# One VectorE instruction over two PSUM banks for the row maxima of the first layer

## The chip, the cores and the metric

The kernel runs on one core of one Trainium2 chip. The metric is the device time of one execution in microseconds, the median of several runs. The core has a matmul engine (TensorE, PE in the profile), a vector engine (VectorE, DVE), a scalar engine (ScalarE, ACT), a general one (GpSimd, POOL) and SyncE (SP), which issues most transfers. Matmul results land in PSUM, eight banks of 512 float32 numbers for each of 128 partitions. Each engine works through its own instructions in order; semaphores order the engines among each other.

## The reference, cut to what matters

Input x is 8 batches of 512 tokens of width 128. Two layers follow one another; each is attention, multiplied by a gate that a mixture of experts gives, and added to x:

```
x  = x0
xn = layernorm(x);  s = attention_0(xn);  g = silu(experts_0(xn));  x = x + s * g
xn = layernorm(x);  s = attention_1(xn);  g = silu(experts_1(xn));  x = x + s * g
```

attention_0 has 16 heads of width 8 with no mask: 8 heads on the first half of xn, 8 on a smoothed copy of the second input (a fixed linear map over time, the Holt smoothing), each a softmax over 512 keys, then a projection, two layer norms and a feed-forward part. attention_1 has 16 causal heads with a linear bias. A softmax needs, for each query row and head, the maximum of 512 scores before the exponentials.

## The kernel before, in words

Attention goes in batch steps b = -2 to 16 (`batches`, `plan`), written out as a list of named steps that all engines follow in the same order. In a step b the kernel makes three kinds of work side by side. First, the **scores** of batch b: a score unit is one head's transposed scores, keys by queries, one 128 x 512 matmul into a bank (L582), an exponential of it by ScalarE (L771), and, for every four units, a sum over keys by eight matmuls (L623). Second, the **maxima** of batch b + 1: a max unit is one head and one tile of 128 query rows, a 128 x 512 matmul into a bank (L589), and a `tensor_reduce` by VectorE that writes the negated maximum of the 512 numbers into one column of `neg_max` (L876). The maxima are later carried into the operands of the next batch's scores (`minus`, `shift`). Third, **other steps**: projections, transposes, layer norms, feed-forward, routing, gathers. They share one bank, `ps_misc`.

In the first layer a batch has 64 score units and 64 max units (`UNITS[0]`), one of each in every `unit` step. Max units 2k and 2k + 1 of a half are the same tile of query rows, for a head of the upper set (j = 1) and its partner in the lower set (j = 0) (`max_unit`). First-layer maxima are made in the eight batch steps b = -1 to 6, those of b = -1 without scores beside them; experts_0 runs between b = 0 and b = 1, experts_1 much later. `plan` puts the sums and the other steps behind units of even number (`(place + 1) * units <= (u + 2) * PLACES`, with 64 units and 32 places; sums stand at u = 4g + 6). So on TensorE an odd unit and the even one after it follow one another with nothing between them, and the sum and the other steps come behind that.

Banks: 0 to 2 are a ring for the scores, 3 to 5 a ring for the maxima (`RING` = 3, `MAX_BANK` = 3), 6 holds the sums, 7 is `ps_misc`. In b = -1 the maxima have banks 2 to 5. TensorE takes the bank of max unit n (n counts over all batches) when `max_out` has reached n - 2, which says that unit n - 3 is reduced: `wait(pe, sems["max_out"], n.at("max_out") - ahead)`, `ahead` = 2; in b = -1 `ahead` is 3. This wait stands in front of both matmuls of the `unit` step, the score's too. VectorE waits for `max_in` to reach n + 1, reduces, and raises `max_out` by 1. `adds` is the table by which every engine counts the semaphores' values as the list goes on.

Of the kernel before, what the change touches and what calls it, by code (L numbers as in the profile page):

```python
# [10 lines left out]
ALU = mybir.AluOpType  # L11
ACT = mybir.ActivationFunctionType
AX = mybir.AxisListType
# [4 lines left out]
QT = S // P  # L18
# [105 lines left out]
def wait(eng, sem, value):  # L124

    if value > 0:
        eng.wait_ge(sem, value)
# [10 lines left out]
BANKS, RING, MAX_BANK, SUM_BANK, MISC_BANK = 8, 3, 3, 6, 7  # L138
# [102 lines left out]
    return half, j, [(first + k, 1, 0, 2 * P, 2 * P * k) for k in range(2)]  # L241


def sums_of(layer):


    if layer == 0:
        return {4 * g + 3: g for g in range(H)}
    return {10 * u + last: 3 * u + k for u in range(QUADS) for k, last in enumerate((3, 7, 9))}
# [88 lines left out]
def adds(step):  # L338

    name, d, arg, layer = step  # L340
    both = {"misc": 1, "misc_free": 1}
    if name == "unit":
        return {**({"scores": 1, "probs": 1} if arg[0] is not None else {}), **({"max_in": 1, "max_out": 1} if arg[1] is not None else {})}
    if name == "fetch":
        return {f"strips{arg[0]}": 16 * (4 + 4 * arg[1])}
    table = {
        "load": {"z_in": 16}, "loadx": {"x_in": 16}, "sum": {"summed": 1}, "take": {"taken": 1},
        "norm": {**both, "dve": 1}, "zTa": {}, "zT": both,
        "q": {**both, "split": 1, "pool": 3, "q_out": 16 * PARTS}, "k": {**both, "split": 1, "pool": 3, "k_out": 16 * PARTS},
        "v": both, "z": both, "shift": {**both, "shift_in": 64}, "minus": {"dve": 1, "minus": 1},  # L350
        "onT": both, "yT": both, "ff1": both, "x2T": both, "logits": both,
        "proj": both, "pmom": {"dve": 1, **({"moments": 1, "rstd": 1, "pool": 1} if arg == 1 else {})},
        "fmom": {"dve": 1, **({"moments": 1, "rstd": 1, "pool": 1} if arg == 1 else {})},
        "ln1": {"pool": 3, "y": 1, "yb": 1}, "ff2a": {},
        "ff2": both,
        "ln2": {"pool": 2, "s": 1}, "gather": {"rows": 16 * QT * (1 if layer == 0 else TOP)},
        "gate": {"gate_in": 1, "pool": 0 if layer == 0 else 1}, "tanh": {"gate_tanh": 1}, "gz": {"gate_out": 1},
        "mix": {"pool": 1, "x2": 1}, "store": {"x2_out": 16}, "tail_take": {"tail_taken": 1},
        "tail_norm": {"tail_norm_in": 1, "tail_norm": 1, "dve": 1}, "tail_turn": {"tail_turn_in": 1, "tail_turn": 1},
        "tail_out": {"tail_out_in": 1, "tail_free": 1, "x2": 1, "x2_out": 16},  # L360
        "ln3a": {"dve": 1, "moments": 1, "rstd": 1, "pool": 1}, "ln3b": {"xn2": 1},
        "gates": {}, "rstd0": {}, "choose0": {}, "count0": {}, "scan0": {}, "slots0": {}, "weigh0": {}, "send0": {}, "wide": {}, "fold": both,
        "positions": {}, "masks": {}, "rest": {}, "choose": {}, "count": both, "place": {}, "weigh": {}, "send": {},
    }
    return table[name]
# [17 lines left out]
def attention(nc, const, psum, banks, strips, tokens, xn2, work, dram, weights, routes, out, setup_of, experts_of):  # L383


    with ExitStack() as ctx:
# [58 lines left out]
        with nc.Block() as block:  # L445
# [76 lines left out]
            def _(pe):  # L522
                n = Tally(adds)
# [26 lines left out]
                for b, steps in batches():  # L550
# [12 lines left out]
                    for step in steps:  # L563
# [3 lines left out]
                        if name == "unit":  # L567
# [4 lines left out]
                            half, jm, max_pieces = max_unit(mi, max_layer) if mi is not None else (0, 1, [])  # L572

                            ahead = RING - 1
                            if b == -1:
                                mbank, ahead = banks[:, 2 + n.at("max_in") % 4, :], 3
                                if mi == 0:
                                    setup["logits_ready"](pe)

# [251 lines left out]
            def _(dve):  # L831
# [20 lines left out]
                for b, steps in batches():  # L852
# [10 lines left out]
                    for step in steps:  # L863
# [3 lines left out]
                        linked[0] = 0  # L867
                        if name == "unit" and arg[1] is not None:
                            _, mi, max_layer = arg
                            bank = banks[:, 2 + n.at("max_in") % 4 if b == -1 else MAX_BANK + n.at("max_in") % RING, :]  # L870
                            half, j, pieces = max_unit(mi, max_layer)
                            slot, qt, *_ = pieces[0]
                            hd, e = QT * j + slot % QT, mi % 10
                            wait(dve, sems["max_in"], n.at("max_in") + 1)
                            if max_layer == 0:
                                dve.tensor_reduce(neg_max[:, half, qt, hd:hd + 1], bank, AX.X, ALU.max, negate=True).then_inc(sems["max_out"], 1)  # L876
                            else:

                                wait(dve, sems["max_out"], n.at("max_out") - 1)
                                for i, (_, qt, lo, hi, at) in enumerate(pieces):  # L880
                                    best = neg_max[:, half, qt, hd + (i if e >= 8 else 0):hd + (i if e >= 8 else 0) + 1]
                                    op = dve.tensor_tensor_reduce(masked[:, n.at("max_in") % 2, at:at + hi - lo], bank[:, at:at + hi - lo],  # L882
                                                                  const["mask_wide"][:, S - (hi - lo):S], -1.0, BIG, ALU.add, ALU.min, best)
                                op.then_inc(sems["max_out"], 1)
# [1218 lines left out]
```

## Time and profile before

| | |
|---|---|
| median of 3 runs | 1211.7 us (1206.21 to 1215.12) |
| profiled execution, its own time | 1209.44 us |
| its span, first to last instruction | 1207.6 us |
| mean granted TensorE clock | 0.912 |
| PE busy | 1022.9 us, 7484 matmuls |
| DVE busy | 794.5 us, 2469 instructions |
| ACT busy | 649.1 us |
| POOL busy | 577.0 us |
| reduces of L876 | 512, 323.8 us busy, 681 ns each |

A line of the profile names the source line, the engine, the tile written and the tile read. "Idle before" is the time for which the engine sat idle just ahead of the instruction, with what released it. A busy share is an average: an engine that is busy two thirds of the time can still be what another engine waits for at a given place.

### The profile page before, as it was taken

How to read it: one execution, taken by the hardware profiler on the slowest of the kernel's cores; microseconds unless marked ns; L12 is line 12 of the kernel's file. 1: busy time of each engine (PE TensorE's matmuls, PEld its weight loads, DVE VectorE, ACT ScalarE, POOL GpSimd, SP SyncE). 2: the span in 40 equal slices, each digit the busy share in tenths (PEclk: the TensorE clock that was granted, in tenths of full speed). 3: DMA queues.
4: the chain of work that ended last, by engine and by line, in shares of the span. 5: the costliest groups of instructions: out<-in, count | busy, mean ns of one | idle time of the engine just before them, and what ended most of it. 6: DMA issues, size and time to landing. Idle time of an engine off the chain costs nothing. (4 is left out here: it accounts for less than half of the span.)

```text
span 1207.6 us, 22982 instructions
## 1 busy us (share of the span) xinstructions
PE 1022.9 (85%) x7484; PEld 547.3 (45%) x7484; DVE 794.5 (66%) x2469; ACT 649.1 (54%) x1255; POOL 577.0 (48%) x670
## 2 busy tenths in 40 slices
PE   4888589998989898887887877786999998899797
PEld 2622149733333333332333343444899754454343
DVE  5597463488878787877776565765444486788631
ACT  1204352376757676665675544444444476677665
POOL 5274500064637373728758578643000165455654
PEclk8657699999999999997998887878999999999978
DMA  5852337681404050412422224124788644354221
GB/s 143 233 136 61 95 114 215 187 210 39 105 22 116 6 128 15 102 31 63 100 62 69 49 64 104 40 79 122 228 254 245 182 109 104 81 136 109 69 53 44
DMA packets 122552, 130.53 MB, mean 108 GB/s; under 512 B 13968, under 2 KB 105424, under 8 KB 122224
## 3 DMA queue, kind: packets, MB, share of 16 engines
q1 hardware_dynamic: 115872, 116.09, 37.0%
q0 software_dynamic: 6144, 12.60, 4.1%
q8 instruction: 58, 0.95, 0.3%
q10 hardware_dynamic: 432, 0.52, 0.2%
q14 instruction: 46, 0.38, 0.1%
HBM read 83.13 MB, written 52.48 MB: 112 GB/s over the span
## 5 line engine op out<-in xcount | busy, mean ns | idle before, releaser
L876 DVE TENSOR_REDUCE a_neg_max<-ps_banks 128x1 f32<-128x512 f32 x512 | 323.8, 681 | 88.2 <-PE ps_banks L589 70.6
L771 ACT ACTIVATE a_probs<-ps_banks 128x512 f32<-128x512 f32 x512 | 279.2, 599 | 154.5 <-PE ps_banks L582 138.1
L582 PE MATMUL ps_banks<-q_strip,k_strip 53*128 53x512 bf16 (+3 forms) x1024 | 281.5, 356 | 74.0 <-DVE a_neg_max L876 30.9
L589 PE MATMUL ps_banks<-k_strip,q_strip 51*128 51x512 bf16 (+3 forms) x1024 | 301.7, 364 | 20.5 <-DVE a_neg_max L876 17.0
L882 DVE CUSTOM_DVE_ANT_0 a_masked<-ps_banks,mask_wide 128x384 bf16<-128x384 f32 (+3 forms) x512 | 223.8, 487 | 91.4 <-PE ps_banks L589 73.4
L773 ACT ACTIVATE a_probs<-ps_banks 128x512 f32<-128x512 f32 x256 | 144.5, 600 | 82.2 <-PE ps_banks L540 69.8
L1062 POOL DMA_INDIRECT tokens<-made,at x96 | 93.3, 972 | 177.6 <-DMA made<-work 126.6
L582 PEld LDWEIGHTS ps_banks<-q_strip,k_strip 53*128 53x128 bf16 x1024 | 72.2, 95 | 164.9 <-issue 62.6
L623 PE MATMUL ps_banks<-a_probs,v_aug 128*32 128x512 f32 x1024 | 143.6, 634 | 0.4
L589 PEld LDWEIGHTS ps_banks<-k_strip,q_strip 51*128 51x128 bf16 x1024 | 74.1, 95 | 142.8 <-ACT a_probs L771 57.8
L1988 POOL DMA_INDIRECT sent<-xn,at x64 | 62.4, 975 | 41.5 <-DMA sent<-xn,at 24.0
L1021 POOL CAST a_q_parts<-a_q_whole 128x512 bf16<-128x512 f32 x16 | 9.8, 610 | 150.3 <-ACT a_q_whole L812 150.3
L539 PE MATMUL ps_banks<-mask_kq,ident_halves 64*128 64x256 bf16 (+1 forms) x320 | 80.1, 262 | 0.3 <-issue 0.3
L1787 PE MATMUL ps_banks<-work 128*128 128x256 f32 x320 | 78.7, 390 | 0.3 <-DMA work<-in_pack 0.2
L1970 DVE SCALAR_TENSOR_TENSOR work<-ps_banks,work 128x256 f32<-128x256 f32 x80 | 35.0, 479 | 64.8 <-ACT work L1824 56.5
L628 PE MATMUL ps_banks<-a_probs,v_aug 128*32 128x512 f32 (+2 forms) x768 | 76.9, 507 | 0.1
L540 PE MATMUL ps_banks<-mask_kq,ident_halves 64*128 64x128 bf16 (+1 forms) x320 | 66.0, 212 | 0.1
L1824 ACT ACTIVATE work<-ps_banks,work 128x256 f32<-128x256 f32 x80 | 33.5, 470 | 56.8 <-PE ps_banks L1787 56.7
L1787 PEld LDWEIGHTS ps_banks<-work 128*128 128x128 f32 x320 | 58.8, 194 | 7.8 <-DMA work<-in_pack 0.9
L775 ACT ACTIVATE a_probs_c<-ps_banks 128x512 f32<-128x512 f32 x64 | 36.5, 595 | 29.2 <-PE ps_banks L540 22.0
L909 DVE RECIPROCAL a_o_den<-ps_banks 128x16 f32<-128x16 f32 x63 | 16.0, 254 | 49.8 <-PE ps_banks L634 35.8
L720 PE MATMUL ps_banks<-work,w_ff 128*128 128x256 f32 x128 | 39.3, 433 | 8.6 <-ACT work L816 5.0
(258 smaller groups left out, 1719.3 us busy)
## 6 DMA issues: line engine op xcount, KB each, us to landing
work<-in_pack SPq DMA_DIRECT2D x40, 450.0 KB, 3.5
q_rows<-a_q_parts SPq DMA_DIRECT2D x96, 128.0 KB
k_rows<-a_k_parts SPq DMA_DIRECT2D x96, 128.0 KB
q_strip<-q_rows SPq DMA_DIRECT2D x64, 192.0 KB
k_strip<-k_rows SPq DMA_DIRECT2D x64, 192.0 KB
work<-in_w SPq DMA_DIRECT2D x32, 256.0 KB, 3.1
sent<-in_zeros SPq DMA_DIRECT2D x14, 512.0 KB, 7.9
work<-sent SPq DMA_DIRECT2D x56, 128.0 KB, 3.3
```

Of the source, the lines that this page charges most:

```text
L539: return pe.matmul(blocks, half_ident(j, half), triangle, start=False, stop=last)
L540: return pe.matmul(blocks[:, :, to], half_ident(j, half), triangle[:, :, src], start=False, stop=last)
L582: mm = pe.matmul(sbank[:, at:at + hi - lo], k_now[rows(js, ROW_END), slot, kt * P:(kt + 1) * P], q_now[rows(js, ROW_END), slot, lo:hi], st ...
L589: mm = pe.matmul(mbank[:, at:at + hi - lo], q_next[rows(jm, ROW_SHIFT), slot, qt * P:(qt + 1) * P], k_next[rows(jm, ROW_SHIFT), slot, lo:h ...
L623: mm = pe.matmul(out_of[c], v_of[k][c], probs[group % 2][:, c, :], start=k == 0, stop=k == QT - 1)
L628: mm = pe.matmul(out_of[c][:, lo:S], v_of[kt][c], kept[:, c, at:at + S - lo], start=kt == 0, stop=kt == 2)
L771: act.activation(probs[si // 4 % 2][:, si % 4, :], bank, ACT.Exp).then_inc(sems["probs"], 1)
L773: act.activation(probs[e // 4][:, e % 4, :], bank, ACT.Exp).then_inc(sems["probs"], 1)
L876: dve.tensor_reduce(neg_max[:, half, qt, hd:hd + 1], bank, AX.X, ALU.max, negate=True).then_inc(sems["max_out"], 1)
L882: op = dve.tensor_tensor_reduce(masked[:, n.at("max_in") % 2, at:at + hi - lo], bank[:, at:at + hi - lo], const["mask_wide"][:, S - (hi - ...
L1062: pool.indirect_dma_start(rows[:, t, :], None, moe[layer], bass.IndirectOffsetOnAxis(ap=routes[layer]["at"][i][:, QT * at + t:QT * at + t ...
L1787: mm = pe.matmul(hidden_bank(par, i)[:, c, :], pack[par][:, (i * FC1 + c) * P:(i * FC1 + c + 1) * P], rows_T[par][:], start=True, stop=True)
```

## The change

In the first layer the even max unit of a pair is no longer reduced when it is written. At the odd unit one `tensor_reduce` reads both banks (128 x 2 x 512) and writes two columns of `neg_max`, four apart, and raises `max_out` by 2. With a ring of three banks the pairs fall on banks (3, 4), (5, 3) and (4, 5) in turn; the pair on (5, 3) keeps its two single reduces (`apart`), and the first of these raises nothing. In b = -1 the pairs lie on (2, 3) and (4, 5), and all are taken together. On TensorE, `ahead` becomes 0 for the odd unit of a pair: it waits until all pairs before its own are reduced. The even unit waits until the pair before the last is reduced, since `max_out` now grows at odd units alone. In b = -1 `ahead` is 2 for both. The second layer's maxima are as before.

```diff
--- before.py
+++ after.py
@@ -239,6 +239,11 @@
     if e < 8:
         return half, j, [(slot, 2, 0, 3 * P, 0), (slot, 0, 0, P, 3 * P)]
     return half, j, [(first + k, 1, 0, 2 * P, 2 * P * k) for k in range(2)]
+
+
+def paired(arg):
+
+    return arg[1] is not None and arg[2] == 0
 
 
 def sums_of(layer):
@@ -340,7 +345,7 @@
     name, d, arg, layer = step
     both = {"misc": 1, "misc_free": 1}
     if name == "unit":
-        return {**({"scores": 1, "probs": 1} if arg[0] is not None else {}), **({"max_in": 1, "max_out": 1} if arg[1] is not None else {})}
+        return {**({"scores": 1, "probs": 1} if arg[0] is not None else {}), **({"max_in": 1, "max_out": 2 * (arg[1] % 2) if paired(arg) else 1} if arg[1] is not None else {})}
     if name == "fetch":
         return {f"strips{arg[0]}": 16 * (4 + 4 * arg[1])}
     table = {
@@ -572,8 +577,10 @@
                             half, jm, max_pieces = max_unit(mi, max_layer) if mi is not None else (0, 1, [])
 
                             ahead = RING - 1
+                            if paired(arg) and mi % 2 == 1:
+                                ahead = 0
                             if b == -1:
-                                mbank, ahead = banks[:, 2 + n.at("max_in") % 4, :], 3
+                                mbank, ahead = banks[:, 2 + n.at("max_in") % 4, :], 2
                                 if mi == 0:
                                     setup["logits_ready"](pe)
 
@@ -867,15 +874,23 @@
                         linked[0] = 0
                         if name == "unit" and arg[1] is not None:
                             _, mi, max_layer = arg
-                            bank = banks[:, 2 + n.at("max_in") % 4 if b == -1 else MAX_BANK + n.at("max_in") % RING, :]
+                            bank = banks[:, MAX_BANK + n.at("max_in") % RING, :]
                             half, j, pieces = max_unit(mi, max_layer)
                             slot, qt, *_ = pieces[0]
                             hd, e = QT * j + slot % QT, mi % 10
-                            wait(dve, sems["max_in"], n.at("max_in") + 1)
-                            if max_layer == 0:
-                                dve.tensor_reduce(neg_max[:, half, qt, hd:hd + 1], bank, AX.X, ALU.max, negate=True).then_inc(sems["max_out"], 1)
+                            at = 2 + n.at("max_in") % 4 if b == -1 else MAX_BANK + n.at("max_in") % RING
+                            if paired(arg):
+                                second = mi % 2 == 1
+                                apart = (MAX_BANK + RING - 1 == at and not second or MAX_BANK == at and second) and b >= 0
+                                if second or apart:
+                                    wait(dve, sems["max_in"], n.at("max_in") + 1)
+                                    if apart:
+                                        op = dve.tensor_reduce(neg_max[:, half, qt, hd:hd + 1], banks[:, at, :], AX.X, ALU.max, negate=True)
+                                    else:
+                                        op = dve.tensor_reduce(neg_max[:, half, qt, QT + slot % QT::-QT], banks[:, at - 1:at + 1, :], AX.X, ALU.max, negate=True)
+                                    op.then_inc(sems["max_out"], 2) if second else None
                             else:
-
+                                wait(dve, sems["max_in"], n.at("max_in") + 1)
                                 wait(dve, sems["max_out"], n.at("max_out") - 1)
                                 for i, (_, qt, lo, hi, at) in enumerate(pieces):
                                     best = neg_max[:, half, qt, hd + (i if e >= 8 else 0):hd + (i if e >= 8 else 0) + 1]
```

## Rows read from the trace of the kernel before

**Rows 1.** The profile's page: busy time by engine; the chain that ended last, by engine.

```profile
PE 1022.9 (85%) x7484; PEld 547.3 (45%) x7484; DVE 794.5 (66%) x2469; ACT 649.1 (54%) x1255; POOL 577.0 (48%) x670
...
PE 19%; issue 4%; DVE 3%; POOL 3%; ACT 1%; DMA 1%; another core or an unknown queue 1%; POOLq 0%; SPq 0%; ACTq 0%; DVEq 0%
```

**Rows 2.** Busy time by stage, its columns first: steps b = -1, 0, 2.

```profile
core 0: us, PE busy (x) PEld busy (x) DVE busy (x) ACT busy (x) POOL busy (x), PEclk, DMA share, GB/s
45.60:100.00 54.40, 41.07 (x104) 12.06 (x104) 48.63 (x91) 4.70 (x7) 32.70 (x37) 0.59 0.60 171
101.00:167.00 66.00, 49.33 (x300) 14.31 (x300) 42.29 (x74) 37.97 (x72) 25.88 (x28) 0.82 0.33 92
...
292.20:356.60 64.40, 57.97 (x390) 23.75 (x388) 51.52 (x120) 43.31 (x82) 35.35 (x38) 0.97 0.29 67
```

**Rows 3.** Waits of step b = 2: waiter <- releaser: us in total, times, longest.

```profile
PEld ps_banks L589 <- ACT a_probs L771: 6.1, 13, 0.8
PEld ps_banks L582 <- ACT a_probs L771: 5.4, 5, 1.7
...
PE ps_banks L582 <- DVE a_neg_max L876: 2.6, 4, 1.1
```

**Rows 4.** VectorE's instructions grouped by line and shape: busy us, mean ns | idle before.

```profile
L876 DVE TENSOR_REDUCE a_neg_max<-ps_banks 128x1 f32<-128x512 f32 x512 | 323.8, 681 | 88.2 <-PE ps_banks L589 70.6 <-remote 10.1 <-issue 4.3
L882 DVE CUSTOM_DVE_ANT_0 a_masked<-ps_banks,mask_wide 128x512 bf16<-128x512 f32 x128 | 84.9, 687 | 36.5 <-PE ps_banks L589 31.7 <-issue 4.0
...
L882 DVE CUSTOM_DVE_ANT_0 a_masked<-ps_banks,mask_wide 128x256 bf16<-128x256 f32 x128 | 47.7, 420 | 22.8 <-PE ps_banks L589 15.8 <-issue 5.2 <-remote 1.6
...
L1123 DVE TENSOR_REDUCE work<-work 128x32 f32<-128x512 f32 x1 | 0.7, 676 | 0.0
```

**Rows 5.** Timeline, step b = -1: start us, us, instruction, count [idle before].

```profile
83.47 6.66 DVE L876 TENSOR_REDUCE a_neg_max<-ps_banks 128x1 f32<-128x512 f32 x11
```

**Rows 6.** Timeline, TensorE and VectorE: one clean pass, then one release.

```profile
273.29 0.39 PE L589 MATMUL ps_banks<-k_strip,q_strip 51*128 51x512 bf16 x1
...
273.71 1.29 DVE L876 TENSOR_REDUCE a_neg_max<-ps_banks 128x1 f32<-128x512 f32 x2 [1.31 <-PE ps_banks L589]
...
319.50 0.68 DVE L876 TENSOR_REDUCE a_neg_max<-ps_banks 128x1 f32<-128x512 f32 x1
...
320.32 0.37 PE L589 MATMUL ps_banks<-k_strip,q_strip 51*128 51x512 bf16 x1 [0.21 <-DVE a_neg_max L876]
```

**Rows 7.** Timeline, TensorE, step b = 2: first and last odd max matmul of 32.

```profile
293.12 0.39 PE L589 MATMUL ps_banks<-k_strip,q_strip 51*128 51x512 bf16 x1
...
356.44 0.39 PE L589 MATMUL ps_banks<-k_strip,q_strip 51*128 51x512 bf16 x1
```

**Rows 8.** Timeline, TensorE, step b = 2: odd max matmuls between 316 and 324.

```profile
316.78 0.39 PE L589 MATMUL ps_banks<-k_strip,q_strip 51*128 51x512 bf16 x1
...
317.90 0.39 PE L589 MATMUL ps_banks<-k_strip,q_strip 51*128 51x512 bf16 x1
...
319.44 0.39 PE L589 MATMUL ps_banks<-k_strip,q_strip 51*128 51x512 bf16 x1
...
322.24 0.39 PE L589 MATMUL ps_banks<-k_strip,q_strip 51*128 51x512 bf16 x1
...
323.37 0.39 PE L589 MATMUL ps_banks<-k_strip,q_strip 51*128 51x512 bf16 x1
```

**Rows 9.** Timeline, VectorE and TensorE, end of step b = 2.

```profile
350.50 0.39 PE L589 MATMUL ps_banks<-k_strip,q_strip 51*128 51x512 bf16 x1
350.73 0.59 PE L589 MATMUL ps_banks<-k_strip,q_strip 51*128 51x512 bf16 x2
...
351.71 5.85 DVE L876 TENSOR_REDUCE a_neg_max<-ps_banks 128x1 f32<-128x512 f32 x9
...
352.54 0.37 PE L582 MATMUL ps_banks<-q_strip,k_strip 53*128 53x512 bf16 x1 [1.21 <-ACT a_probs L771]
```

**Rows 10.** Waits of TensorE between 120 and 143 us.

```profile
PE ps_banks L582 <- issue: 9.8, 3, 6.3
```

## The prediction

> **What bounds the kernel now.** I read the page first. PE is busy for 85% of the span, VectorE for 66%, and the chain that ended last runs mostly through PE and hardly through VectorE [rows 1]. So a saving on VectorE is worth only what it gives where PE waits for VectorE. Then I read busy time by stage. Step b = 2, typical of b = 1 to 6, takes 64.4 us: PE 58.0, VectorE 51.5, ScalarE 43.3. Step b = -1 has no scores: VectorE has 48.6 of 54.4 us and PE 41.1 [rows 2]. So VectorE leads in one short step, and PE in the long ones. Third, the waits of b = 2. PE waits there for VectorE's reduces for only 2.6 us; its weight loads wait 11.5 us (6.1 + 5.4) for exponentials [rows 3]. Last, the timeline of single passes, to see how far apart the odd max matmuls stand, since the change hangs a new wait on them.
>
> **What the merge saves on VectorE.** A single reduce takes 681 ns; a custom pass over PSUM takes 687 ns for 512 numbers and 420 for 256 [rows 4], so 256 numbers cost 267 ns, and 512 cost 534. A reduce of 1024 should take 681 + 534 = 1215 ns (estimate). No reduce over two banks is in the trace. The cheap bound is this one; the dear one is two full reduces, 1362 ns. I take 1215, as a reduce into 32 results takes 676 ns for 512 numbers [rows 4], so further rows of results cost nothing.
>
> The saving is less than 1362 - 1215 = 147 ns, however. Eleven reduces in a row take 6.66 us [rows 5]: the last lasts 0.68, so ten spacings take 5.98, 0.60 us each, and each reduce starts 0.08 before the one in front ends. Two cost 1.21 us of the queue and the merged one 1.215 - 0.08 = 1.14: 0.07 us saved. The Trainium skill (VectorE: DVE Perf Modes, The DRAIN you can't avoid) says that the next op does not start until the pipe has emptied. By that rule the saving would be the full 0.147. The trace disagrees: its starts are 0.60 apart and the duration 0.68.
>
> Merged are all 32 pairs of b = -1. Of the 224 pairs of b = 0 to 6 the 74 on banks 5 and 3 stay single and 150 are merged. VectorE's saving is 182 x 0.07 = 13 us in all. On the path lies b = -1 alone, 32 x 0.07 = 2.3 us, if everything behind it moves up too. Bounds there: nothing, as step b = 0 has a stall in which PE waits up to 6.3 us at once with nothing on VectorE or ScalarE that releases it [rows 10], which may swallow the gain; and 32 x 0.147 = 4.7. I take 2. The looser or tighter waits of b = -1 (four banks, two pairs) cost nothing as long as PE refills two banks inside the 1.14 us of the other pair; if not, a few tenths per pair, at most some 5 us.
>
> **What the new wait costs.** Today the even unit may be reduced while PE does something else, and a bank comes free three units later. After the change the next odd unit waits until the pair before it is wholly reduced, and that reduce can't begin before the last odd matmul is through. The loop from one odd max matmul to the next is therefore: matmul start to reduce start 0.42 us (273.29 to 273.71), the reduce of both banks 1.215, and the release: a reduce ends at 319.50 + 0.68 = 320.18 and the matmul starts at 320.32, 0.14 [rows 6]. Sum 1.78 us. For a pair left single the loop is 0.42 + 0.68 + 0.14 = 1.24. These are floors; the score matmul of the odd unit stands behind the same wait, and the even unit, the sum and all other steps stand behind it on PE. ScalarE, which waits for scores, and GpSimd and the SP queue, fed by `ps_misc` steps, get everything later.
>
> Now the spacings of today. In b = 2 there are 32 odd max matmuls, at 293.12 first and 356.44 last [rows 7], so 63.3 / 31 = 2.04 us apart on average, above the floor. But they are uneven. Between 316.78 and 323.37 they are 1.12, 1.54, then (with the one at 320.32 of [rows 6]) 0.88, 1.92 and 1.13 apart [rows 6, 8]. The floors there, by bank, are 1.78, 1.78, 1.24, 1.78, 1.78: shortfalls 0.66, 0.24, 0.36, 0 and 0.65, 1.9 us. Over all 31 spacings of b = 2 I count 10 under their floor, 5.9 us short. The same count gives 5.5, 6.9, 5.5, 4.4 and 7.3 for b = 1 and 3 to 6, together 35.5 us, and 6.9 for the part of b = 0 behind its stall: 42.4 us. What is short before the stall I cost at nothing, as the stall hides it; without that cover it is 2 to 3 us more.
>
> Not all of it stays. At the end of b = 2 two odd units are 0.45 apart (350.50 and the second of the two at 350.73), 1.33 us short, but PE then waits 1.21 us for an exponential [rows 9], and a PE that comes later waits less. In the stretch of [rows 8] no such wait is left and 1.9 us stay. If I let every gap between PE's matmuls take up lateness that has piled up, walking through the seven steps leaves 15 us; if about a third is taken up, as in these two samples together, 27 us. I take the middle, 21, since some of the gaps are waits on chains that move along. Bounds: 0 and 42.
>
> Other VectorE work delays the pair's reduce (norm, z, moments, about ten pieces of 0.3 to 0.7 us in a step); most stand in the long spacings, so I cost them at nothing, bounded by 1 us per step, 6 us.
>
> **The two rules on grouping.** In b = 2 VectorE is busy 80% of the stage and a queue of nine reduces back to back exists [rows 2, 9], yet PE seldom waits for it. The Trainium skill (Perfetto Trace Analysis, Optimizing Scalar/DVE Operations) says that grouping helps when the engine is saturated, and that where it is not but causes bubbles on others, breaking up instructions may let work finish sooner. Its first half speaks for the change and describes the second rival; the second half speaks against it and describes my forecast.
>
> **Sum.** 1209.4 us, the profiled execution's own time (span 1207.6), - 2 + 21 = 1228.4. The median of the runs stood 2.3 above that execution, so I forecast 1231 us.
>
> **Rivals.** *Absorbed.* PE's 11.5 us of waits for exponentials per step [rows 3] exceed the 5.9 us short; if ScalarE sets the pace, later scores cost nothing as long as ScalarE has one in hand. For it: the ends of the steps [rows 9]. Against it: in [rows 8] the spacing is shorter than 1.24 because PE has nothing to wait for. Time: 0 to 10 us over, 1210 to 1222. Chance 0.22.
>
> *VectorE is the limit after all.* The mechanism: in stretches where reduces run back to back (nine in 5.85 us [rows 9]), VectorE's queue sets PE's pace, and a shorter queue lets PE go on. The price is 0.07 us for a merged pair, 13 us in all: 1198 us. It decides where the queue of VectorE, other work included, is longer than 1.78 us per pair, since the loop above is then hidden. At 51.5 us per 32 pairs [rows 2] it is 1.61 on average, so only in parts. By the skill's rule on the drain, in the part above, the saving would be 27 us and the time 1185. Chance 0.12, 0.09 of it over 1% faster.
>
> *Nothing is taken up.* ScalarE starves when the odd unit's score comes late and pushes its own lateness on, and other VectorE work lengthens the loop: 42 + 6 - 0 = 48 us at most, 1245 to 1260. Chance 0.16.
>
> *The merged instruction does not do what it says,* that is, two banks cost like two reduces: loop 1.93 instead of 1.78, some 4 us more. It is inside the range.
>
> **How the numbers follow.** The forecast, 1222 to 1245, has 0.50. The range 1207 to 1252 takes in the absorbed case and half of the last; about 0.1 lies under it and 0.08 over it. A measurement of this kernel can tell about 1% (12 us) from no change: 1199.6 to 1223.8 is "same". Faster 0.09; same 0.27 (0.20 absorbed, 0.03 from the faster case, 0.04 from the forecast's edge); slower 0.64.
>
> **What the profile after would show.** L876 has 330 instructions, 182 of them with a mean near 1.21 us; if near 1.36, the saving is wrong. Spacings of odd max matmuls are hardly ever under 1.24, and under 1.78 only at single pairs; waits of L582 and L589 for L876 in b = 2 rise from 2.6 us to 6 or more, waits for exponentials fall. Steps b = 1 to 6 are each 2 to 5 us longer, b = -1 1 to 2 shorter, experts_0, experts_1 and the second layer the same. If the steps keep their length while the waits rise, the work was absorbed. If waits for L876 fall, I am wrong from the start.

## The result, and the profile after

The changed kernel takes 1257.6 us (median of 4 runs, 1256.9 to 1259.4) against 1213.4 for the kernel before: ratio 1.0377, 95% interval 1.033 to 1.0424. It is 44 us slower; I had forecast 19 (-2 + 21).

The page after, first part and the two groups of the first layer's reduces:

```profile
PE 1029.8 (82%) x7484; PEld 556.1 (44%) x7484; DVE 783.6 (62%) x2287; ACT 653.1 (52%) x1255; POOL 577.5 (46%) x670
...
L890 DVE TENSOR_REDUCE a_neg_max<-ps_banks 128x2 f32<-128x1024 f32 x182 | 220.6, 1222 | 123.0 <-PE ps_banks L596 107.4
...
L888 DVE TENSOR_REDUCE a_neg_max<-ps_banks 128x1 f32<-128x512 f32 x148 | 100.8, 683 | 18.5 <-PE ps_banks L596 14.7
```

They answer to [rows 1, 4]. The instruction does what it says: 182 merged reduces of 1.222 us, against my 1.215, and VectorE has 10.9 us less to do, against my 13. Its idle time ahead of these reduces has grown from 88.2 us [rows 4] to 141.5 (123.0 + 18.5), and the part of it that a max matmul ended from 70.6 to 122.1: VectorE waits more and works less.

Busy time by stage in the changed kernel (columns as in [rows 2]): steps b = -1, 0, 2, then b = 1 to 6 together, then all that follows the first layer's maxima:

```profile
45.60:95.00 49.40, 28.64 (x104) 9.81 (x103) 46.35 (x60) 4.70 (x7) 32.24 (x37) 0.60 0.67 190
96.30:173.00 76.70, 49.28 (x300) 15.32 (x300) 41.14 (x51) 38.90 (x72) 25.91 (x28) 0.82 0.30 84
...
305.50:379.30 73.80, 61.94 (x390) 24.65 (x388) 50.84 (x98) 43.76 (x82) 34.30 (x36) 0.89 0.27 62
...
237.30:672.20 434.90, 357.72 (x2310) 146.24 (x2312) 302.01 (x576) 262.03 (x492) 223.63 (x249) 0.93 0.30 72
...
672.60:1257.00 584.40, 505.05 (x4240) 304.66 (x4236) 351.88 (x1463) 322.67 (x638) 275.29 (x333) 0.91 0.43 113
```

The same two long stretches in the kernel before, which were not among the rows ahead:

```profile
231.50:620.30 388.80, 343.58 (x2310) 139.09 (x2312) 309.23 (x704) 258.74 (x492) 219.83 (x246) 0.97 0.34 81
...
620.70:1207.00 586.30, 499.99 (x4238) 301.79 (x4235) 352.65 (x1463) 322.88 (x638) 278.69 (x336) 0.92 0.43 113
```

These rows show where the 50 us between the two spans lie. Steps b = 1 to 6 grew from 388.8 to 434.9, 46 us. Step b = 0 grew by 10 to 11, b = -1 shrank by 4 to 5, experts_0 is as it was, and everything behind is 2 us shorter. The granted clock in b = 1 to 6 fell from 0.97 to 0.93.

Waits of step b = 2 in the changed kernel (as [rows 3]):

```profile
PE ps_banks L596 <- DVE a_neg_max L890: 6.8, 8, 1.9
PE ps_banks L596 <- DVE a_neg_max L888: 2.1, 2, 1.3
...
PEld ps_banks L596 <- ACT a_probs L778: 15.0, 16, 2.4
...
ACT a_probs L778 <- PE ps_banks L589: 21.7, 18, 2.8
```

PE's waits for reduces rose from 3.0 us (the 2.6 of [rows 3] and 0.4 at L589) to 8.9. The weight loads' waits for exponentials, which I had expected to fall, rose from 11.5 to 15.0 us. A part of these 15.0 us belongs to the same places: at 364.7 us the weight load's wait of 1.70 is put down to an exponential, and the wait of the matmul behind it, 1.34, to a reduce. ScalarE's waits for score matmuls rose to 21.7 us; in the kernel before they were

```profile
ACT a_probs L771 <- PE ps_banks L582: 13.9, 14, 2.6
```

One pass of the loop in the changed kernel, first the line of VectorE, then PE's timeline:

```profile
332.07 1.23 DVE L890 TENSOR_REDUCE a_neg_max<-ps_banks 128x2 f32<-128x1024 f32 x1 [0.20 <-PE ps_banks L596]
```

```profile
331.58 0.39 PE L596 MATMUL ps_banks<-k_strip,q_strip 51*128 51x512 bf16 x1
...
333.44 0.37 PE L596 MATMUL ps_banks<-k_strip,q_strip 51*128 51x512 bf16 x1 [0.67 <-DVE a_neg_max L890]
...
335.29 0.37 PE L596 MATMUL ps_banks<-k_strip,q_strip 51*128 51x512 bf16 x1 [0.25 <-DVE a_neg_max L890]
336.61 0.37 PE L596 MATMUL ps_banks<-k_strip,q_strip 51*128 51x512 bf16 x1 [0.71 <-DVE a_neg_max L888]
```

The odd max matmul starts at 331.58, the merged reduce at 332.07 (0.49 later) and ends at 333.30, and the next odd max matmul starts at 333.44, 0.14 after. That is a spacing of 1.86; the next is 1.85, and 1.32 where the pair is reduced by single instructions. In steps b = 0 to 6 no spacing is under 1.31 us, while in the kernel before they went down to 0.44. The floors of my forecast were 1.78 and 1.24. The difference is the start of the reduce after its matmul: 0.42 in the kernel before (63 of its 186 spacings), 0.48 to 0.49 here; no run shows why.

Of the signs that I had named, the 330 reduces, the floors and the stages that changed are there. But steps b = 1 to 6 are each 6 to 9 us longer, not 2 to 5.

### The profile page after: what moved, and what is told of

It reads as the page before. It is cut to its first block and busy times, and to the rows that moved or that the text cites. A ratio compares the mean times of both kernels' runs of the same rounds, so it can differ in the third digit from the quotient of the medians.

```text
span 1257.5 us, 23049 instructions
## 1 busy us (share of the span) xinstructions
PE 1029.8 (82%) x7484; PEld 556.1 (44%) x7484; DVE 783.6 (62%) x2287; ACT 653.1 (52%) x1255; POOL 577.5 (46%) x670
## 5 line engine op out<-in xcount | busy, mean ns | idle before, releaser
L596 PE MATMUL ps_banks<-k_strip,q_strip 51*128 51x512 bf16 (+3 forms) x1024 | 290.7, 370 | 117.3 <-DVE a_neg_max L890 79.8
L589 PE MATMUL ps_banks<-q_strip,k_strip 53*128 53x512 bf16 (+3 forms) x1024 | 280.9, 362 | 32.3 <-DVE a_neg_max L897 14.7
L890 DVE TENSOR_REDUCE a_neg_max<-ps_banks 128x2 f32<-128x1024 f32 x182 | 220.6, 1222 | 123.0 <-PE ps_banks L596 107.4
L630 PE MATMUL ps_banks<-a_probs,v_aug 128*32 128x512 f32 x1024 | 150.4, 662 | 0.0
L589 PEld LDWEIGHTS ps_banks<-q_strip,k_strip 53*128 53x128 bf16 x1024 | 74.9, 95 | 108.9 <-ACT a_probs L780 52.0
L888 DVE TENSOR_REDUCE a_neg_max<-ps_banks 128x1 f32<-128x512 f32 x148 | 100.8, 683 | 18.5 <-PE ps_banks L596 14.7
L2003 POOL DMA_INDIRECT sent<-xn,at x64 | 62.6, 978 | 44.4 <-DMA sent<-xn,at 26.9
```

The source lines that it names most:

```text
L589: mm = pe.matmul(sbank[:, at:at + hi - lo], k_now[rows(js, ROW_END), slot, kt * P:(kt + 1) * P], q_now[rows(js, ROW_END), slot, lo:hi], st ...
L596: mm = pe.matmul(mbank[:, at:at + hi - lo], q_next[rows(jm, ROW_SHIFT), slot, qt * P:(qt + 1) * P], k_next[rows(jm, ROW_SHIFT), slot, lo:h ...
L630: mm = pe.matmul(out_of[c], v_of[k][c], probs[group % 2][:, c, :], start=k == 0, stop=k == QT - 1)
L888: op = dve.tensor_reduce(neg_max[:, half, qt, hd:hd + 1], banks[:, at, :], AX.X, ALU.max, negate=True)
L890: op = dve.tensor_reduce(neg_max[:, half, qt, QT + slot % QT::-QT], banks[:, at - 1:at + 1, :], AX.X, ALU.max, negate=True)
```

## The experiments

They ran on chips of two speeds: the kernel before takes 1170 us on the faster ones and 1213 to 1226 on the others, where PE stalls in b = 0 for some 17 us that the faster ones do not lose. So ratios are told, each against the kernel before on its own chip, and stage times are given for b = 1 to 6, which take the same time on both (386.0 and 388.8 us in the kernel before). A stage time comes from the one profiled execution of a kernel, a ratio from all its executions. Columns: "at half clock" is the time in b = 1 to 6 for which the granted clock stood at 1.2 GHz. The theories: **1**, the loop from an odd max matmul over the reduce of the pair to the next odd max matmul makes the loss; **2**, putting reduces off to the odd unit costs by itself; **3**, the instruction over two banks is to blame; **4**, scores held behind the wait starve ScalarE; **5**, the granted clock; **6**, other VectorE work in the loop.

| kernel | ratio, 95% interval | b = 1 to 6, us | at half clock in it, us |
|---|---|---|---|
| before (c0) | 1 | 386.0 | 20.5 |
| changed (first comparison) | 1.0377, 1.033 to 1.0424 | 434.8 | 59.5 |
| changed again (c1) | 1.0411, 1.034 to 1.0483 | 435.1 | 61.4 |
| e1 release by pair | 1.0067, 1.0036 to 1.0098 | 393.6 | 20.5 |
| e2 two at odd | 1.0347, 1.0292 to 1.0402 | 433.1 | 70.8 |
| e3 first step only | 0.9996, 0.9971 to 1.0021 | 388.4 | 27.3 |
| e4 score ahead | 1.0279, 1.0229 to 1.0329 | 417.0 | 35.4 |
| e5 four banks, merged | 1.035, 1.0309 to 1.039 | 418.2 | 47.8 |
| e6 four banks, single | 1.0125, 1.0095 to 1.0155 | 391.2 | 10.2 |
| e7 half read, merged | 0.9902, 0.9864 to 0.9941 | 387.5 | 27.3 |
| e9 half read, single | 0.9875, 0.9822 to 0.9928 | 386.7 | 20.5 |
| e10 four banks, aligned, merged | 1.0243, 1.0191 to 1.0296 | 399.0 | 10.2 |
| e11 four banks, aligned, single | 1.0261, 1.0197 to 1.0325 | 396.6 | 13.7 |
| e15 score ahead again | 1.0267, 1.0233 to 1.0302 | 417.0 | 35.4 |
| e12 filler | 1.0317, 1.0281 to 1.0353 | 420.7 | 23.9 |
| e8 first step, score ahead | 0.9972, 0.9953 to 0.9992 | 386.3 | 20.5 |
| changed, third time (c2) | 1.0407, 1.0352 to 1.0462 | 434.8 | 55.6 |
| e16 more VectorE work, merged | 1.0667, 1.0606 to 1.0728 | 466.4 | 85.3 |
| e17 more VectorE work, single | 1.0227, 1.0174 to 1.028 | 423.7 | 44.4 |

**c0, c1, c2: the two kernels again.**

> The kernel before, unchanged, for its profile beside the other kernels of this call on the same chip. All theories: the same time as the runs of before, steps b = 1 and 2 from first to last max matmul 60.5 and 63 to 64 us.

> The changed kernel, unchanged, timed on the chip of these experiments, so that its ratio and its stage times stand beside theirs. Theory 1 (the loop): the same 1.035 to 1.04 as in the first comparison; the step b = 0 has no stall on this chip, and nothing in the theory hangs on that stall. Rival: a part of the first loss belonged to the stall, 1.02 to 1.03 here.

> The changed kernel, unchanged, as the base of e16 on this chip: 1.035 to 1.04 of before.

c0 took 1166.5 us in its one execution; seven others of the kernel before on that chip took 1169.2 to 1175.2, so it is 0.4% under their median. c1 and c2 gave 1.0411 and 1.0407; c1 ran on the slower chips. e2, which differs from the changed kernel by 0.06 us a pair, gave 1.0347 where b = 0 has no stall, so the loss does not hang on the stall.

**e1: single reduces, release by pairs.** In the changed kernel's VectorE part:

```diff
+ wait(dve, sems["max_in"], n.at("max_in") + 1)
+ op = dve.tensor_reduce(neg_max[:, half, qt, hd:hd + 1], banks[:, at, :], AX.X, ALU.max, negate=True)
+ op.then_inc(sems["max_out"], 2) if second else None
- (single or merged reduce, at the odd unit)
```

> Every max unit is reduced by its own instruction as soon as it is written, as in the kernel before; TensorE's waits and the release of banks by pairs are those of the changed kernel. The loop from one odd max matmul to the next is then 0.48 + 0.68 + 0.15 = 1.31 us for all pairs, where the changed kernel shows 0.48 + 1.22 + 0.15 = 1.85. Theory 1, the length of the loop makes the loss: spacings of the kernel before fall under 1.31 by some 2 to 3 us in a step, so 1213 + 10 to 20, 1223 to 1235, and no spacing under 1.31. Theory 2, releasing by pairs is what costs, whatever the reduce takes: 1250 or more. Theory 3, the single reduce over two banks is to blame and nothing else: 1213.

1.0067, 7.2 us by the medians, b = 1 to 6 7.6 us longer than c0; least spacing 1.32. Theory 2 in its form "release by pairs costs whatever the reduce takes" falls, and so does theory 3 in its strict form, which had 1 here. Theory 1's range was 10 to 20 us, a little high.

**e2: both maxima at the odd unit, by two instructions.**

```diff
- op = dve.tensor_reduce(neg_max[:, half, qt, QT + slot % QT::-QT], banks[:, at - 1:at + 1, :], AX.X, ALU.max, negate=True)
+ if not apart:
+     dve.tensor_reduce(neg_max[:, half, qt, hd + QT:hd + QT + 1], banks[:, at - 1, :], AX.X, ALU.max, negate=True)
+ op = dve.tensor_reduce(neg_max[:, half, qt, hd:hd + 1], banks[:, at, :], AX.X, ALU.max, negate=True)
```

> The changed kernel with its merged instruction taken apart again: both maxima of a pair are reduced at the odd unit by two instructions back to back, 0.60 + 0.68 = 1.28 instead of 1.22 us. Waits, order and release stay as changed. Theory 1 (loop length) and theory 2 (release by pairs): as slow as the changed kernel or a little slower, 1258 to 1270, of which about 2 to 3 in step b = -1 and 0.06 for each of about 85 pairs whose loop binds. Theory 3 (the instruction over two banks is to blame): 1213 to 1225.

1.0347. The merged instruction is not to blame: without it the loss is the same. Busy time of b = 1 to 6, one row each from c0, e1 and e2 (us of the stretch, PE, weight loads, VectorE, ScalarE, GpSimd, clock):

```profile
214.60:600.50 385.90, 343.20 (x2308) 139.30 (x2308) 308.27 (x704) 258.85 (x492) 220.15 (x246) 0.97 0.34 82
```

```profile
213.30:606.90 393.60, 340.61 (x2308) 140.38 (x2308) 308.96 (x704) 260.26 (x492) 221.07 (x246) 0.97 0.33 80
```

```profile
221.80:655.00 433.20, 362.22 (x2310) 146.06 (x2310) 308.02 (x703) 261.73 (x492) 223.25 (x249) 0.92 0.30 73
```

VectorE is busy for 308 to 309 us in all three, with 703 or 704 instructions. Only when the reduces may start differs, and that is worth 40 us between e1 and e2 in these profiles. By the medians it is 35 us, since the profiled execution of e2 was the slowest of its four (1220.1 us, median 1212.9).

**e3: merged in b = -1 alone.** `paired` asks for `arg[0] is None` as well, and b = 0 to 6 are as before.

> The merged instruction in step b = -1 alone, where there are four banks and no scores; from b = 0 on everything is as in the kernel before. In the changed kernel b = -1 is 4.4 us shorter from its first to its last max matmul. If step b = 0 takes that over: 1209, 4 to 5 us less than before. If the stall in the middle of b = 0 (GpSimd sends tokens out one after another) swallows it: the same as before within 1 us. Either way the whole loss is in b = 0 to 6.

0.9996: nothing that this run can tell, which is about 3 us. The 4.4 us by which b = -1 was shorter in the first profile are not the merge's either: b = -1 took 52.8 us before, 48.3 in the first profile after, 53.4 in c1 and 53.6 in c2 (between its first and last max matmul), and 49.9 in c0 against 49.0 in e3.

**e4, e15: the score's matmul ahead of the wait.**

In the changed kernel both matmuls of a unit stand behind the wait. In e4 and e15 (the lines that matter):

```diff
+ if early:                       # a score and a first-layer maximum in the unit
+     score_piece(0)
  wait(pe, sems["max_out"], n.at("max_out") - ahead)
+ if early:
+     max_piece(0)
```

> The changed kernel with one order turned: in a first-layer unit TensorE issues the score's matmul before it waits for the bank of the maxima, so that the score is not held behind that wait. Theory 4, the loss is made worse by ScalarE running dry behind the held scores (its waits for scores rose from 13.9 to 21.7 us in step b = 2): 1240 to 1250. Theory 1 alone (loop of maxima): 1255 to 1258, since the odd max matmuls keep their floor of 1.85 us and set the pace.

> e4 (changed kernel, score's matmul ahead of the wait for the maxima's bank) once more, as the control of e12 on the same chip: 1.025 to 1.03 of before, and TensorE at half clock for some 40 us of steps b = 1 to 6.

1.0279 and 1.0267, inside what theory 4 had expected: b = 1 to 6 take 417.0 us instead of 434.8, so 18 us come back in the stages. By the medians it is less: e4 is 9.6 us faster than e2 on the same chip. ScalarE's waits for scores in b = 2 are 19.3 instead of 21.7 us, and time at half clock fell from 60 to 35 us. The edit does a second thing: the spacings behind merged pairs now sit on a floor of 1.77 to 1.81 instead of 1.85, as the max matmul starts 0.06 us after the reduce's end and not 0.15. Counted as in my prediction, the spacings of the kernel before are 34.9 us under floors of 1.77 and 1.24, and 40.0 under 1.85 and 1.32; so some 5 of the 18 us may be the shorter loop and not the earlier score (estimate).

**e5, e6: four banks for the maxima, two for the scores.** In both `sbank = banks[:, n.at("scores") % 2, :]`, `mbank = banks[:, 2 + n.at("max_in") % 4, :]`, `wait(pe, sems["probs"], n.at("probs") - 1)`; e5 merges all pairs (`ahead = 2`), e6 none (`ahead = 3`).

> The changed kernel with four banks for the maxima in every step (banks 2 to 5, as in b = -1) and two for the scores (0 and 1). All pairs are merged, and a unit waits for the pair before the last, not for the last. Theory 1, the loop: the floor is 1.85 us for two pairs, that is 0.93 a pair, and no longer binds; what is left is the price of the missing score bank, which e6 measures by itself. e5 and e6 are then within 1% of each other. Theory 2, reduces put off to the odd unit cost by themselves (they stand behind other VectorE work, and the maxima are ready later): e5 is slower than e6 by 2% or more.

> The kernel before with the same banks as e5: two for the scores, four for the maxima, each unit reduced by itself and released by itself. It measures the price of the missing score bank: a score waits for the exponential two units before it. Theory of scores that run dry: 3% or more slower than before. Otherwise, as four banks for the maxima give back some of PE's waits for reduces (2.6 us in a step): within 1%.

1.035 and 1.0125. By my expectation the distance between them spoke for theory 2; e6 by itself lies between the 1% and the 3% that I had put down for it. But the floor that I had written down for e5 was wrong. PE's timeline of e5 at the end of step b = 3:

```profile
417.23 0.37 PE L586 MATMUL ps_banks<-q_strip,k_strip 53*128 53x512 bf16 x1 [1.07 <-DVE a_neg_max L887]
...
419.25 0.60 PE L593 MATMUL ps_banks<-k_strip,q_strip 51*128 51x512 bf16 x1
```

The matmul that waits at 417.23 is the score of an even unit, and it waits for a reduce. The even unit 2k + 2 follows the odd unit 2k + 1 at once and needs the bank of pair k - 1, whose odd half was written one burst earlier. So the loop binds there too, at another place. The matmul at 419.25 takes 0.60 us, where [rows 6] have 0.39 for the same: the granted clock has fallen (the profile has it at 1.2 GHz from 417.8 us on).

**e10, e11: the same banks, and other steps behind odd units.** `(place + 1) * units <= (u + 1) * PLACES` for all steps, and sums four units after their last exponential instead of three.

> e5 with another order of steps: sums and other steps stand behind odd units instead of even ones, so that both units of a pair follow one another on TensorE. In e5 the even unit that follows an odd one waits for the pair that the odd unit of the burst before completed, so the loop of 1.85 us still stood between bursts, in spite of four banks. Here a burst waits for the pair of the burst before the last. Theory 1 (the loop): e10 and e11 within 0.5% of each other. Theory 2 (a reduce put off costs by itself, as VectorE idles for half of the pair): e10 is slower than e11 by 1 to 2%, as e5 than e6 (1.035 and 1.0125).

> e6 with the order of steps of e10: the control without the merge. The order itself may cost or give something against e6 (1.0125): the score behind each burst now has two exponentials to wait for at once, so 1.01 to 1.03.

1.0243 and 1.0261; b = 1 to 6 take 399.0 and 396.6 us, and 2.2 of the 2.4 us between them lie in b = 6. In step b = 3 the 31 spacings of the two kernels are the same to 0.01 us but for one, 2.76 against 2.87, though all pairs are merged in one and none in the other. With the loop out of the way a reduce put off to the odd unit costs nothing that these runs can tell (to some 0.5%); theory 2 falls here. Both kernels lose 2.5% to the order and the missing score bank, most of it outside these steps.

**e7, e9: half of each bank is read,** `0:S // 2` in place of the whole bank, in the changed kernel and in the kernel before.

> The changed kernel, but each reduce of the first layer reads 256 of the 512 scores of a bank, so the maxima are those of half of the keys. The merged reduce then takes 0.68 us, as a single one did, and the loop 0.48 + 0.68 + 0.15 = 1.31 us as in e1, while the reduces are still put off to the odd unit and still stand behind other VectorE work. Theory 1, length of the loop: as e1, ratio 1.00 to 1.01. Theory 2, the order on VectorE: the loss stays to a good part, 1.02 or more.

> The kernel before, but each reduce of the first layer reads 256 of the 512 scores of a bank, so the maxima are those of half of the keys. It is the control for e7 (changed kernel, half read, 0.990): it has the short reduces without the merge and without the wait. If VectorE's own time matters in the kernel before (its reduces now 0.42 instead of 0.68 us), 0.98 to 0.985, and then e7's put-off reduces still cost 0.5 to 1%. If it hardly matters apart from step b = -1: 0.99, the same as e7, and with a loop of 1.31 us the merge costs nothing.

0.9902 and 0.9875. A merged reduce of 2 x 256 numbers (0.690 us) makes the loop as short as e1's, and b = 1 to 6 take 387.5 us merged and 386.7 single, as much as the kernel before. The merge, the waits by pairs and the order on VectorE are all there in e7; only the length of the loop is not. The shorter reduces lighten VectorE too, but they do so in both kernels, which end up alike. The ratio under 1 is not the loop's: in e7 step b = -1 takes 41.0 us against 49.9 in c0, which is about what e7 gains; e9 gains 15 us, of which its b = -1 (46.2 us) explains a part, and the rest was not placed.

**e12: filler in the waits.** e15 with the score's matmul of odd units issued three times from unit 47 of a step on.

```diff
+ for _ in range(2 if mi % 2 == 1 and mi >= 47 else 0):
+     pe.matmul(sbank, ...)       # the same product, before score_piece(0)
```

> e15 with filler on TensorE: from max unit 47 of a first-layer step on, the score's matmul of the odd unit is issued three times instead of once, into the same bank, before the wait (the last one counts; the result is the same). That is 54 times 0.43 us or more of TensorE work in places where it mostly waits. Theory 5, a part of the loss is the granted clock, which falls to half where TensorE idles in the loop: less time at half clock in steps b = 1 to 6 and a ratio 0.005 to 0.01 below e15. Theory 1 alone, or a clock that does not follow idling: the filler is hidden or costs, e15 plus 0 to 10 us, and the time at half clock stays.

1.0317 against 1.0267 for e15. Time at half clock fell from 35.4 to 23.9 us, and still the kernel is no faster. That is neither of the two outcomes that I had written down. In step b = 3 one spacing fell from 2.64 to 1.77, where the clock had been at half, and three rose, 2.52 to 2.95 the most, where the filler was not hidden. The filler did change the time at half clock, but the run doesn't price it. A rough price comes from two profiles of the same kernel: step b = 3 of the changed kernel took 68.9 us in the first and 70.7 in c1,

```profile
379.30:448.40 69.10, 58.57 (x390) 24.27 (x386) 48.37 (x91) 43.76 (x82) 33.57 (x36) 0.97 0.26 59
```

```profile
381.70:452.50 70.80, 60.95 (x390) 24.55 (x388) 48.51 (x91) 43.73 (x82) 33.81 (x36) 0.91 0.27 60
```

with 4.7 and 12.8 us at half clock: 1.8 us for 8.1, about 0.22 a microsecond. The executions on record say the same: among those of one kernel on one chip, 148 in 23 groups, the time rises by 0.21 us for each microsecond at half clock, taken from their mean granted clocks. For the 39 us more at half clock (59.5 against 20.5) that is some 8 us of the 46, an estimate, and neither source tells whether the clock made an execution longer or the longer waits lowered the clock.

**e16, e17: more VectorE work,** `dve.tensor_reduce(spare[i][:], ps_misc, AX.X, ALU.max)` ahead of norm, z, proj and ff2 in b = 1 to 6.

> The changed kernel with seven more VectorE instructions in each of steps b = 1 to 6: a reduce of ps_misc (0.6 us of VectorE's queue) into one spare column ahead of norm (4), z, proj and ff2; the results don't change. 4.2 us a step, 25 in all. Theory 6: other VectorE work that stands ahead of a pair's reduce lengthens the loop of 1.85 us and reaches TensorE one to one where the loop binds (95 of 186 spacings), and this made some 26 us of the measured loss. Then e16 is slower than c2 by 13 to 25 us, and clearly more than e17 is slower than before. Rival: VectorE has slack and the loss is the bare loop: e16 and e17 rise alike, by less than 8 us.

> The kernel before with the same seven instructions a step. It measures what they cost where each unit is reduced and released by itself: the ring of three takes up much of it. Theory 6: 1.003 to 1.01 of before (4 to 12 us), less than in the changed kernel. Rival: the same rise as in e16.

1.0667 and 1.0227: by the medians 30 us more than c2, and 25 more than before. In b = 1 to 6 it is 31.6 and 34.9 us. Neither kernel takes up any of the added 25 us. The added work stands ahead of the release of `ps_misc`, for which PE waits in either kernel, so it tests that release too and not the pair's alone. Theory 6, that other VectorE work weighs more in the changed kernel, is not confirmed; e17's 4 to 12 us was plainly wrong, and e16's 13 to 25 was too low.

**e8: the harmless parts alone,** e3 and e4's edits on the kernel before.

> The kernel before with the two parts that did no harm by themselves: merged reduces in b = -1 (e3: 0.9996) and the score's matmul ahead of the wait for the maxima's bank (worth 0.7% in the changed kernel, e4 against c1). TensorE waits for reduces for only 2.6 us in a step of the kernel before, so at most 1 us a step comes back: 0.993 to 1.00. Rival: the score ahead of the odd max matmul delays the maxima and VectorE: 1.00 to 1.005.

0.9972, 0.9953 to 0.9992: 3 to 4 us faster than the kernel before. As e3 gave nothing, it is likely the score's place; the two parts were not told apart at this size.

## Why the prediction was wrong

The direction, the mechanism and its place were right: the loop, its floor, the steps in which it binds, and the other stages unchanged. What the merge saves on VectorE was nearly right too (10.9 us less busy for my 13, none of it on the path). The size was off by 2.3 times, and the time lies above the range. The reading of the chain in [rows 1] carried nothing: in the kernel before that chain goes back to 818.6 us only, behind all of the first layer's maxima, so it says nothing of the steps in which the change acts.

**The step that failed is what becomes of the count: "Not all of it stays", 21 us taken off, while other VectorE work ahead of the pair's reduce, "I cost them at nothing", put nothing against it.** The count itself was nearly right. With the measured floors 1.85 and 1.32 instead of 1.78 and 1.24 the same spacings of b = 1 to 6 come 40.0 us short instead of 35.5, and the measured growth of their spacings is 42.9, where half of 35.5 was forecast. So, as a net, all of it stays. The net has parts. In the first profile after, 95 of the 186 spacings are released by a reduce (release within 0.2 us); their reduces start 25.8 us later in sum than 0.49 after their matmul, 11.5 of it in b = 5. Against that, spacings that are shorter after than before make 23.2 us: 40.0 + 25.8 - 23.2 is 42.6. I had bounded the first at 6 us. What was taken up, 23.2, is not less than the 18 that I took off in these steps. One such late start, at the end of b = 2:

```profile
359.25 0.39 PE L596 MATMUL ps_banks<-k_strip,q_strip 51*128 51x512 bf16 x1
...
360.90 0.46 DVE L1373 CAST ident_halves<-consts 64x128 bf16<-64x128 f32 x2
361.39 1.23 DVE L890 TENSOR_REDUCE a_neg_max<-ps_banks 128x2 f32<-128x1024 f32 x1
```

The pair's reduce could start at 359.74 and starts at 361.39, behind seven other VectorE instructions (L945, L1366 to L1373).

**The cause of the size stays open in part.** The late starts alone are not enough: in e1, by the same count, 68 spacings start 25.9 us late in sum, as much as in the changed kernel, and c0's spacings are 19.7 us short of a floor of 1.32 for all pairs, yet e1's grow by 6.5 us only against c0. There 33 us are taken up by shorter spacings, in the changed kernel 23 of a larger sum. By these counts the longer loop does two things that I did not put together: it raises more spacings to its floor, and it leaves less room to make up for them. e16 and e17 do not show that added VectorE work costs the changed kernel more than the one before.

The sample that I took for recovery was the end of b = 2, where PE waited 1.21 us for an exponential [rows 9]. The six last spacings of each step, of 31, hold 18.3 of the 42.9 us: the ends of the steps lose most. PE's wait for ScalarE there was not slack, at least in part because the score that ScalarE needed next stood behind the same wait as the maxima. e4 speaks for that: with the score ahead these last spacings grow by 11.0 us instead of 18.3, though e4's loop is also a little shorter.

**Step b = 0** lost 10.8 us in the first comparison, 9.6 without the stall (e2 against c0), where I had counted 6.9 short and nothing for the part ahead of the stall; with the measured floors the whole step comes 10.6 short. The stall did not hide that part. **The gain of 2 us in b = -1** was not seen, though e3 could not have told 2 us from none.

**The clock** had no term in my sum. It is about 8 us by the estimate above; in e12 the time at half clock fell and the kernel was no faster, so it stays an estimate.

**The rivals.** "Nothing is taken up" (0.16, 1245 to 1260) has the time that came, and both things that it names are there: ScalarE waits longer for scores, and other VectorE work delays the pair's reduce. Its number is in part luck: it had 42 + 6 - 0, and the trace has 40.0 + 25.8 - 23.2 for b = 1 to 6. "Absorbed" and "VectorE is the limit" are out by e1, e2 and e7. The Trainium skill (Perfetto Trace Analysis, Optimizing Scalar/DVE Operations) had it in the half that speaks against the change: where an engine is not saturated but makes others wait, breaking up instructions may let work finish sooner. The runs agree: e1, where each unit is reduced as it comes, has 40 us less in b = 1 to 6 than e2, where both wait for the odd unit. By the rule that I took from the Trainium skill (VectorE: DVE Perf Modes, The DRAIN you can't avoid) merging would have freed 0.147 us of VectorE a pair. I had read that section too narrowly: it also says that an op that is not held starts earlier, and the starts 0.60 us apart [rows 5] agree with that. Measured is 10.9 us over 182 pairs, 0.06 a pair; neither size shows in a time, as no saving of VectorE reached the path.

## What to carry to other kernels

When an instruction is merged over several buffers of a ring, count the loop that the ring has left: producer start to consumer start, the whole merged consumer, and the release. Compare it with the shortest spacings of the producer, not with their mean. The shortfall is no fixed price: of 40 us short all stayed here, of the 20 us of e1's shorter loop about a third. So take all of it as lost for a loop near the mean spacing (1.85 against 2.05), unless a trace shows that what stands behind the same wait has slack of its own. If a merge is wanted, it needs a second full set of buffers, and the producer's bursts must match the merged group, as in e10, where the merge then cost nothing; but that kernel was 2.4% slower than before, by the bank and the order that it took. If something must wait, put the work that others need ahead of the wait.

## What the runs showed of the hardware

- A max reduce over two PSUM banks in one instruction takes 1.222 us for 2 x 512 float32 numbers, 0.683 for 512 in one bank; 2 x 256 numbers over two banks take 0.690 (e7). So the second bank costs next to nothing beyond its numbers.
- From the odd max matmul's start to the start of an idle VectorE's reduce is 0.48 to 0.49 us in the changed kernel and in e1, 0.42 in the kernel before. From a reduce's end to the max matmul that it releases is 0.15 in 91 of the 95 spacings it ends; in e4, where the score's matmul is already issued, it is 0.06.
- PE's granted clock fell to 1.2 GHz for stretches mostly at the ends of the steps, where PE had waited in the loop, and in the middle of b = 5 as well: 20.5 us of b = 1 to 6 in the kernel before, 56 to 61 in the changed one, 10 in e6 and e10.
- Two chips run the same kernel in 1170 and 1213 to 1226 us; 17 us of it lie in b = 0 (65.5 against 48.8), and some 23 behind the first layer's maxima (587 against 564), while b = 1 to 6 are the same to 1%. No trace here shows what makes the difference.
